# A normalised two-layer network: two stages change places in VectorE's order, and two in GpSimd's

## The reference

```python
x = x + 0.5 * ffn(layernorm(x))
x = x + attention(layernorm(x))
x = x + 0.5 * ffn(layernorm(x))

# ffn: of each of the 16 groups of 64 hidden units only one is kept
mask_logits = einsum('bl,lxy->bxy', xf @ m1, m2) + mb
quant_mask  = argmax(mask_logits, axis=-1)
mid  = xf @ w1                       # used where the unit is the group's argmax
res  = relu(mid picked) @ w2 + b2
```

## Time and profile before

| | |
|---|---|
| median of three runs | 3364.14 us (3363.8 to 3367.4) |
| the profiled execution | 3363.8 us |
| its span, first to last instruction | 3362.1 us |
| PE busy in the span | 93% |
| DVE busy | 79% |
| ACT busy | 49% |
| POOL busy | 39% |
| granted PE clock, mean | 0.99 |

### The profile page before, as it was taken

How to read it: one execution, slowest core, us unless ns; L and a number is a source line. 1 busy time by engine, 2 the same in 40 slices (tenths; PEclk the granted TensorE clock), 3 DMA queues, 4 the chain that set the end, 5 groups by cost and what they waited for, 6 DMA issues and landing times. The chain is left out here.

```text
span 3362.1 us, 102510 instructions
## 1 busy us (share of the span) xinstructions
PE 3140.9 (93%) x36736; PEld 2710.0 (81%) x36736; DVE 2654.7 (79%) x4369; ACT 1644.0 (49%) x4554; POOL 1313.5 (39%) x2170
## 2 busy tenths in 40 slices
PE   5999999999979999789999999999799999999999
PEld 4888888898865665578887877887688888988888
DVE  7999999999943323278877878877699999999998
ACT  3333333333336556577777777777433333333332
POOL 3333333333323433255555555555433333333332
PEclk9999999999989999899999999999899999999999
DMA  3111111111125555433333333333211111111111
GB/s 85 58 56 52 56 56 56 52 56 56 52 92 196 200 197 195 169 99 103 97 100 103 103 102 97 100 103 103 69 52 56 56 56 51 56 56 54 53 56 46
DMA packets 224965, 290.57 MB, mean 86 GB/s; under 512 B 25460, under 2 KB 191732, under 8 KB 224888
## 3 DMA queue, kind: packets, MB, share of 16 engines
q1 hardware_dynamic: 224888, 289.52, 27.2%
HBM read 171.97 MB, written 117.44 MB: 86 GB/s over the span
## 5 line engine op out<-in xcount | busy, mean ns | idle before, releaser
L578 PE MATMUL mid_ps<-xT_hl,w_hl 128*128 128x128 f16 x12288 | 730.4, 219 | 0.0
L425 PE MATMUL res_ps<-w_hl,midT_hl 128*128 128x256 f16 x6144 | 712.5, 273 | 1.2 <-DVE x_out L546 1.2
L578 PEld LDWEIGHTS mid_ps<-xT_hl,w_hl 128*128 128x128 f16 x12288 | 699.7, 98 | 0.5
L382 POOL TENSOR_TENSOR var_eps<-moments,eps_col 128x1 f32<-128x1 f32 x384 | 110.4, 287 | 1420.0 <-DVE moments L378 1420.0
L425 PEld LDWEIGHTS res_ps<-w_hl,midT_hl 128*128 128x128 f16 x6144 | 590.4, 98 | 65.5 <-DVE midT_hl L533 1.7
L486 ACT ACTIVATE midT_hl<-mid_ps 128x1024 f16<-128x1024 f32 x256 | 261.9, 1023 | 686.4 <-PE mid_ps L589 686.4
L512 DVE TENSOR_TENSOR_SCAN runmax<-restart,logits_ps 128x1024 f32<-128x1024 f32 x256 | 585.5, 2287 | 8.3 <-PE logits_ps L567 0.4
L397 ACT ACTIVATE xn_hl<-xc,rstd 128x256 f16<-128x256 f32 x384 | 194.0, 505 | 475.0 <-POOL rstd L387 386.9
L372 DVE BATCH_NORM_STATS2 stats<-x_in 128x6 f32<-128x256 f32 x384 | 162.0, 422 | 294.0 <-DMA x_in<-x 289.3
L517 DVE TENSOR_TENSOR step<-runmax 128x1024 bf16<-128x1024 f32 x256 | 315.0, 1230 | 8.9
L533 DVE SCALAR_TENSOR_TENSOR midT_hl<-mid_ps,midT_hl 128x1024 f16<-128x1024 f32 x256 | 311.9, 1218 | 7.5 <-ACT midT_hl L486 7.5
(11 more groups left out here) (143 smaller groups left out, 6253.6 us busy)
## 6 DMA issues: line engine op xcount, KB each, us to landing
projected<-qkfv_out SPq DMA_DIRECT2D x128, 512.0 KB, 2.9
qkv<-projected SPq DMA_DIRECT2D x128, 384.0 KB, 3.4
x<-x_out SPq DMA_DIRECT2D x256, 128.0 KB, 1.7
x_in<-x SPq DMA_DIRECT2D x256, 128.0 KB, 2.2
x_res<-x SPq DMA_DIRECT2D x256, 128.0 KB, 2.1
x_in<-in_L_attn_x SPq DMA_DIRECT2D x128, 128.0 KB, 2.1
x_res<-in_L_attn_x SPq DMA_DIRECT2D x128, 128.0 KB, 2.1
gate<-projected SPq DMA_DIRECT2D x128, 128.0 KB, 3.1
```

The lines of the kernel that those rows point to most:

```text
L425: last = nc.tensor.matmul(dst, left(lp, k), right(rp, k), start=(k == 0 and lp == rp), stop=(k == blocks - 1 and lp == 1))
L578: nc.tensor.matmul(mid_ps[t.slot][:, cols], w1_hl[:, wp, k, cols], xT_hl[:, t.ring, xp, k], start=(c % PER_BANK == 0 and k == 0 and wp == xp),
```

## The change

In the ffn phase, POOL's list has `centre` of tile s+5 ahead of `add_bias` of tile s-1, where it was behind it. DVE's list has `first_max` of tile s+1 ahead of `low_low` of tile s+2. Nothing is added or removed, and PE's, ACT's and SP's programs are the same.

```diff
-                    pipeline(pool, [(add_bias, -1), (lambda t: norm.centre(pool, t), 5)],
+                    pipeline(pool, [(lambda t: norm.centre(pool, t), 5), (add_bias, -1)],
                              tiles, base, UNROLL, LONGEST_LAG)

-                    pipeline(dve, [(finish, -2), (lambda t: norm.stats(dve, t), 5), (low_low, 2),
-                                   (first_max, 1), (reached, 1),
+                    pipeline(dve, [(finish, -2), (lambda t: norm.stats(dve, t), 5),
+                                   (first_max, 1), (low_low, 2), (reached, 1),
                                    (lambda t: norm.aggregate(dve, t), 5), (lambda t: norm.low(dve, t), 4),
                                    (reject, 1), (mid_low, 0)],
                              tiles, base, UNROLL, LONGEST_LAG)
```

## The result

| | before | after |
|---|---|---|
| median of the runs | 3365.77 us (4 runs, 3363.8 to 3369.44) | 3422.59 us (4 runs, 3420.39 to 3427.73) |
| the profiled execution | 3363.8 us | 3423.29 us |
| its span | 3362.1 us | 3421.5 us |

The change made the kernel slower: ratio 1.0170, 95% interval 1.0152 to 1.0187, some 57 us. The forecast was 3439 us, in a range of 3395 to 3455.

A forecast was written before the change was run, and what follows sets the result against it. PE, at 7.17 us a step, was taken as the bound before; the changed order closes a ring of 7.48 us. The two phases' +37.9 and +37.4, together +75, on 3363.8 give 3439 us, range 3395 to 3455.

The forecast's parts named there:

- DVE's gap: Ffn step, DVE ahead of L539, waiting for low_hl: 0.42 us, which goes but by itself gives nothing in the steady stretch.
- a ring through DVE and POOL: Ffn: x_out waits for the bias, that for POOL's centre, that for DVE's moments, behind the x_out before; one turn per step.
- The ring's length: Sum of the distances in one turn in the ffn: 7.48 us, bounds 7.19 to 7.55, against PE's 7.17.
- the tails: The last six tiles of a phase, with no centre before their bias: they run at PE's pace, change 0.
- stats to the scan: On DVE, from the stats' start to the scan's: its duration 0.42 and a start gap of 0.03, 0.45 us.
- The other terms: Finish to stats 0.33, scan onward 2.32, low_low to L517 0.32, L517 to aggregate 1.15, aggregate to bias end 2.83, handover 0.08.
- DVE's idle time ahead of x_out: DVE ahead of L546 in each of about 244 ffn steps: some 0.7 us, released by POOL's x_res L474.
- The starts: Start of each ffn phase, where waits for low_hl go from the scans' way: a gain of 1.9 us, bounds 0 and 3.2.
- PE waits ahead of L412: PE ahead of its transposes in the ffn: about 0.3 us idle a step, released by DVE's low_hl L539.
- The first rival: No change: with a shorter POOL chain the ring stays below 7.17, at 7.0 to 7.1; 3362 us, chance 0.06.
- The second rival: Faster: DVE and its gap set the step, so losing 0.42 us in 256 steps gives 3256 us; chance 0.02.
- the stacked waits: Third rival: DVE waits for the bias and PE for low_low, adding up to 7.90 us a step; 3541 us, chance 0.04.

The follow-up runs named there:

- dve_only: The kernel before with only DVE's two stages exchanged, POOL's list as before: 3363.41 us, ratio 0.9996.
- pool_only: The kernel before with only POOL's two stages exchanged, DVE's list as before: 3462.22 us, ratio 1.0280.
- after_low_at_0: The changed kernel with low_low (L539) on partitions 0 to 63 in place of 64 to 127, plus a wait on low_h1_made: 3427.01 us, ratio 1.0182.
- after_bias_twice: The changed kernel with the bias's addition made twice on POOL, first into a spare tile: 3589.26 us, ratio 1.0663.
- after_reject_last: The changed kernel with one more exchange on DVE, reject (L526) behind mid_low (L533): 3466.91 us, ratio 1.0297.
- after_step_half: The changed kernel with DVE's L517, between x_out and the aggregate, over 8 of the 16 groups only: 3363.05 us, ratio 0.9998.
- after_bias_half: The changed kernel with the bias added to only the first 128 of the 256 columns: 3364.43 us, ratio 1.0000.
- after_midlow_half: The changed kernel with DVE's L533, behind the aggregate, over half of its columns: 3423.75 us, ratio 1.0174.

## Why the prediction was right, point by point

- PE bounds the kernel before, and DVE's gap is worth nothing by itself: shown by dve_only. One reading on the way was wrong: POOL is said never to be waited for, but the earlier trace rows has ACT idle 1.77 us for POOL's rstd. What the argument needs is less, that neither DVE nor PE waits for POOL, and that holds.
- The bias in its new place closes a ring through DVE and POOL, one turn per step: shown from all sides, by pool_only, the bias longer and shorter, and the halved instructions.
- The ring's length: 7.48 forecast, 7.41 measured as a mean. Over 242 turns this made 79 us of the forecast's sum, and 62 were measured: 17 too much, with 1.2 more gained in the tails and 2.3 lost outside, which leaves the 16 by which 3439 was too high.
- The term that was off is "stats to the scan", put at 0.45 us by a row with low_low in between; it is 0.33. L539 works on partitions 64 to 127, all its neighbours start at 0, and it and its successor start only when the one ahead has finished, while the others overlap by 0.1 us. The change thus removed one such place from the ring, stats to low_low. The Trainium skill states this ("VectorE: DVE Perf Modes", section "Two Vector instructions with no wait between them", which calls it a model: an instruction is held until all earlier ones are done when an input or its output starts in another quadrant, that is, another group of 32 partitions, than the last one did in the same memory); by that rule the runs with low_low at partition 0 agree, with 0.19 and 0.18 us for the 0.33 behind it.
- The other terms were within 0.02 us. The second wait instruction in three of eight steps, 0.045 us as a mean, was not in the sum and made up for part of the 0.12.
- DVE's idle time ahead of x_out: some 0.7 us forecast, 0.51 to 0.63 measured. The step is 0.07 shorter, and DVE has a third held place that nobody expected: L533, the next behind L539 that reads PSUM, starts 0.73 or 0.74 us after L526 begins, once L526 has ended, in the changed kernel and in dve_only, but 0.62 us after it before the change, in pool_only and in after_low_at_0. It stands behind the aggregate, off the ring, and costs no time.
- The starts: 1.9 us gained per phase forecast, 1.9 measured. In the first ffn that is two small errors against each other: the second stats gained 2.2 and not 2.4 us, as the first scan still waits 0.92 us for its logits, and the chain behind them was 0.1 shorter. The tails gained 0.6 each where 0 was forecast.
- PE waits ahead of L412: so it does, 0.23 us a step for 0.31. The prediction named low_hl as the releaser. In the changed kernel the profile says "issue" in the steady steps, and low_hl where the wait is longer, as in pool_only (0.3 us, in 19 steps) and after_bias_twice (0.69 to 0.84). L412 starts 0.35 us after L539's end in the changed kernel and in pool_only alike, though their steps differ in length, so L539 is what it waits for.
- The first rival asked whether POOL's chain might shorten. Its mechanism is real and can't be used so simply: after_reject_last and after_low_at_0 each freed rstd and lost as much or more elsewhere. The second rival is out by dve_only, and the stacked waits by the idle times: in the steady steps DVE has no gap ahead of L539 or of the scan.

## What to carry to other kernels

Two stages of one engine that exchange places in a software pipeline can take a whole step of slack from a tile, though the order looks the same to the eye. Follow each wait round until it comes back to where it began: if the ring has no tile of slack, its sum of start-to-start distances is a lower bound of the step, whatever the engines' loads are. Only what lies on the ring, or holds up an instruction on it as L526 does POOL's, is worth shortening or moving, and below the busiest engine's own step nothing more is gained.

## What the runs showed of the hardware that was not expected

- Waits ahead of a VectorE instruction cost by where they stand. From the last event to the start of x_out: 0.04 us when the wait is on x_out itself (for the product, in dve_only and after_step_half), 0.09 to 0.13 when it is on a wait instruction right ahead (for the bias), 0.14 when it is on one that also computes a register (for the product, in the same two runs), and 0.21 when such a one stands between the bias's wait and x_out, though its own wait is long over.
- A GpSimd instruction held up by VectorE's L526, 0.70 us long, takes 0.35 to 0.62 us longer: rstd 0.90 for 0.55, the bias 1.24 for 0.72, var_eps 0.96 for 0.34. Which of them is hit hangs on some hundredths of a microsecond: L526 ahead of the bias by 0.05 is enough.
- The start-to-start distances show what durations don't: on partitions 64 to 127 in place of 0 to 63 an instruction of 0.29 us costs 0.11 or 0.12 us more ahead of it and 0.14 or 0.15 behind it.
- The name that the profile gives a wait isn't proof of its cause. One and the same wait for the bias is put down to "issue" or POOL in the changed kernel, and to PE or POOL in after_bias_half, after_midlow_half and after_low_at_0. What tells it is the distance from the bias's end, 0.09 or 0.21 us in each of them.
